# Delta stage: levels whole instead of in halves, leading tokens once per four heads, VectorE's work placed anew

## The reference

```python
q = causal_conv_silu(x @ Wq, conv_q_w, conv_q_b)   # 4 taps in time; k and v the same
g = -jnp.exp(A_log)[None, None, :, None] * jax.nn.softplus(x @ Wfa @ Wfb + dt_bias)
beta = jax.nn.sigmoid(x @ Wb)
q, k = l2norm(q) * SCALE, l2norm(k)

def step(S, inp):
    qt, kt, vt, gt, bt = inp
    S = S * jnp.exp(gt)[..., None]
    vd = (vt - jnp.einsum('bhkv,bhk->bhv', S, kt)) * bt[..., None]
    S = S + kt[..., None] * vd[:, :, None, :]
    return (S, jnp.einsum('bhkv,bhk->bhv', S, qt))
o = o * lax.rsqrt(jnp.mean(o * o, -1) + EPS) * o_norm_w * jax.nn.sigmoid(x @ Wga @ Wgb)
return o.reshape(b, t, D) @ Wo
```

## Time and profile before

| what | value |
|---|---|
| median of 3 runs | 3721.74 us (3715.66 to 3722.37) |
| the profiled execution, its own time | 3717.97 us |
| its span in the profile | 3715.8 us |
| TensorE matmuls busy over the span | 3474.6 us, 94% |
| VectorE busy | 1941.4 us, 52% |
| ScalarE busy | 1427.4 us, 38% |
| GpSimd busy | 125.0 us, 3% |

### The profile page before, as it was taken

The page is one execution under the profiler, slowest core; times in us unless marked ns, Lnnn a source line. Parts: engine busy times, 40 slices in busy tenths (PEclk is TensorE's granted clock), DMA queues, the critical chain, the costliest instruction groups (busy, mean ns, idle before and its releaser), DMA issues. The chain is left out here.

```text
span 3715.8 us, 86134 instructions
## 1 busy us (share of the span) xinstructions
PE 3474.6 (94%) x37416; PEld 1694.5 (46%) x37416; DVE 1941.4 (52%) x3334; ACT 1427.4 (38%) x3313; POOL 125.0 (3%) x457
## 2 busy tenths in 40 slices
PE   6979999996789999999999999999999759999999
PEld 4454444442344544444444444444444435444444
DVE  2131111113778897789878878887888431111111
ACT  1010000001466656666665666566656521000000
POOL 0000000000000000000000000000000000000000
PEclk9979999997989999999999999999999868999999
DMA  4011100003111111121111111111211042000000
GB/s 154 7 57 36 28 0 29 11 0 120 48 31 36 42 50 34 45 66 41 33 56 43 48 50 45 42 37 39 65 39 34 16 154 63 14 15 29 0 12 12
DMA packets 83725, 156.21 MB, mean 42 GB/s; under 512 B 8782, under 2 KB 33998, under 8 KB 79516
## 3 DMA queue, kind: packets, MB, share of 16 engines
q1 hardware_dynamic: 83356, 150.77, 12.3%
HBM read 133.71 MB, written 17.04 MB: 41 GB/s over the span
## 5 line engine op out<-in xcount | busy, mean ns | idle before, releaser
L1333 PE MATMUL psum<-dl_xt,dl_wqkv 128*128 128x512 f32 x1536 | 778.2, 624 | 10.4 <-DVE dl_qkv L977 10.0
L513 DVE SCALAR_TENSOR_TENSOR f_act_g<-psum,f_bup,f_act_g 128x512 f32<-128x512 f32 x96 | 72.1, 751 | 939.4 <-ACT f_act_g L468 939.4
L977 DVE SCALAR_TENSOR_TENSOR dl_qkv<-psum,dl_par,dl_qkv 128x511 f32<-128x511 f32 (+2 forms) x576 | 430.4, 747 | 14.0
L468 ACT ACTIVATE f_act_g<-psum,f_bgate 128x512 f32<-128x512 f32 x96 | 66.0, 687 | 923.1 <-PE psum L411 923.1
L1333 PEld LDWEIGHTS psum<-dl_xt,dl_wqkv 128*128 128x128 f32 x1536 | 257.4, 189 | 250.2 <-issue 212.5
L411 PE MATMUL psum<-xnt_sb,wup 128*128 128x512 f32 x768 | 345.2, 592 | 0.0
L407 PE MATMUL psum<-xnt_sb,wgate 128*128 128x512 f32 x768 | 345.2, 592 | 0.0
L429 PE MATMUL psum<-f_wdown,f_hidden 128*128 128x512 f32 x768 | 344.9, 592 | 0.0
L1340 PE MATMUL psum<-dl_wo,dl_sg 128*128 128x512 f32 x512 | 260.9, 623 | 2.9 <-DVE dl_qkv L977 2.5
L407 PEld LDWEIGHTS psum<-xnt_sb,wgate 128*128 128x128 f32 x768 | 145.9, 190 | 183.7 <-issue 183.7
L411 PEld LDWEIGHTS psum<-xnt_sb,wup 128*128 128x128 f32 x768 | 145.9, 190 | 183.7 <-issue 183.7
(11 more groups left out here) (192 smaller groups left out, 4618.1 us busy)
## 6 DMA issues: line engine op xcount, KB each, us to landing
dl_wqkv<-in_dw_qkv SPq DMA_DIRECT2D x192, 256.0 KB, 2.6
dl_wo<-in_dwo SPq DMA_DIRECT2D x16, 1024.0 KB, 5.2
f_weights_b<-f_weights_by_expert SPq DMA_DIRECT2D x48, 256.0 KB, 6.3
wgate<-in_wgate SPq DMA_DIRECT2D x2, 3072.0 KB, 18.6
wup<-in_wup SPq DMA_DIRECT2D x2, 3072.0 KB, 24.7
f_wdown<-in_wdown SPq DMA_DIRECT2D x2, 3072.0 KB, 13.6
x_sb<-in_x SPq DMA_DIRECT2D x4, 1024.0 KB, 9.3
x_after_experts<-x_sb SPq DMA_DIRECT2D x16, 256.0 KB, 2.0
```

Of the source, the lines that this page charges most:

```text
L977: tap_ = lambda dl: dve.scalar_tensor_tensor(y_[:, dl:TT], ps[:, bank, 0:TT - dl], par[:, h, 4 * a + 3 - dl:4 * a + 4 - dl], y_[:, dl:TT], ...
L1333: last = pe.matmul(ps[:, bank, :], wq[:, n % RING, m, :], xt[:, u // HG % 2, m, :], start=(m == 0), stop=(m == KC - 1))
```

## The change

The level products of a level are issued whole instead of in two halves, at one place of the slot. Their scaling takes all tokens and both parts of `kq` in one instruction (`level_scale`), and the product of the decays is one instruction too (`level_decay`). The wait on `half_level` goes, and `late` counts levels instead of halves. The sums move from the end of slot 8 to its inner place, the cross and corner products to the end of slots 14 and 15. The leading tokens of four heads are added in one instruction after their convolutions (`edges`), for which ScalarE's `silu` now waits; `bnd` is held twice. The series for small arguments has one term less and its threshold is 2^-8 instead of 2^-6. In VectorE's list, the pieces of work get other places before and behind `add_state`; `level_take` of levels 1 to 5 moves from the head of slots 7 to 11 to their tails, `blocks_out` from the tail of slot 11 to the tail of slot 12, and `blocks_in` from the tail of slot 13 to before `add_state` of slot 14.

```diff
-    every, first, second = None, (0, 1), (2, 3)
+    every, quarters = None, (0, 1, 2, 3)
...
-             (6, "states"): [("level", w, 0, first)], (6, "inner"): [("level", w, 0, second)],
-             (6, "split"): [("level", w, 1, first)], (6, "end"): [("level", w, 1, second)],
-             (8, "end"): [("sums", w, 0, every)],
+             (6, "inner"): [("level", w, 0, quarters)], (6, "end"): [("level", w, 1, quarters)],
+             (8, "inner"): [("sums", w, 0, every)],
...
-             (14, "inner"): [("cross", w, 0, first), ("krow", w, 2, every)], (14, "end"): [("cross", w, 0, second)],
-             (15, "inner"): [("vrow", w, 0, every), ("corner", w, 0, first)], (15, "end"): [("corner", w, 0, second)]}
+             (14, "inner"): [("krow", w, 2, every)], (14, "end"): [("cross", w, 0, quarters)],
+             (15, "inner"): [("vrow", w, 0, every)], (15, "end"): [("corner", w, 0, quarters)]}
...
-    if 7 <= sl <= 10 and at in ("inner", "end"):
-        jobs.append(("level", w, sl - 5, first if at == "inner" else second))
+    if 7 <= sl <= 10 and at == "end":
+        jobs.append(("level", w, sl - 5, quarters))
...
                 def silu(u, a, signal):
-                    for j in range(HJ):
-                        wait_read(act, "proj", u, 4 * (1, 0, 2)[a] + j)
+                    act.wait_ge(s["edged"], 3 * u + (2, 1, 3)[a])
                     act.activation(qkv[:, a], qkv[:, a], ACT.Silu).then_inc(signal, 1)
 
...
                     if not late:
-                        if i == 0:
-                            dve.wait_ge(s["bnd_ready"], u + 1)
                         dve.wait_ge(s["tapped"], 12 * u + i + 1)
-                        step(dve.tensor_tensor(y_[:, 0:3], y_[:, 0:3], bnd[:, a, j, :], ALU.add))
                         step(tap_(1))
                         o.done(tap_(2))
                         conv_done[(u, i)] = o.n
...
+                def edges(u, a):
+                    dve.wait_ge(s["bnd_ready"], u + 1)
+                    for j in range(HJ):
+                        wait_read(dve, "proj", u, 4 * (1, 0, 2)[a] + j)
+                    dve.tensor_tensor(qkv[:, a, :, 0:3], qkv[:, a, :, 0:3], bnd(u)[:, a], ALU.add).then_inc(s["edged"], 1)
+
...
-                        o.done(dve.tensor_scalar(poly, w_, -0.25, None, ALU.mult))
+                        o.done(dve.tensor_scalar(poly, w_, 1.0 / 3.0, None, ALU.mult))
                     else:
                         o.wait(mark[("series", u, n - 1)])
-                        ins = dve.scalar_tensor_tensor(poly, poly, (1.0 / 3.0, -0.5, 1.0)[n - 1], w_, ALU.add, ALU.mult)
-                        if n == 3:
-                            ins.then_inc(s["series_done"], 1)
-                        else:
-                            o.done(ins)
+                        o.done(dve.scalar_tensor_tensor(poly, poly, (-0.5, 1.0)[n - 1], w_, ALU.add, ALU.mult))
...
                 def near_zero(u):
                     if u >= 2:
                         dve.wait_ge(s["o_ps"], SLOTS * (u - 1))
-                    o.done(dve.tensor_scalar(flat(kq(u)[:, 1]), flat(sg[:]), 2.0 ** -6, None, ALU.is_lt))
-                    mark[("near", u)] = o.n
+                    o.wait(mark[("series", u, 2)])
+                    dve.tensor_scalar(flat(kq(u)[:, 1]), flat(sg[:]), 2.0 ** -8, None, ALU.is_lt).then_inc(s["series_done"], 1)
...
-                def cut(u, lv, side):
-                    m, hs = 1 << (lv - 1), slice(TT // 2 * side, TT // 2 * side + TT // 2)
-                    segs = lambda ap: ap[:, :, hs].rearrange("p j (n r m) -> p j n r m", r=2, m=m)
-                    return m, segs(qkv[:, KK]), segs(dec)
-
-                def level_early(u, lv, side):
-                    m, kk_, dv = cut(u, lv, side)
-                    nb = TT // (4 * m)
-                    if side == 0:
-                        dve.wait_ge(s["half_level"], (LEVELS + 1) * u + lv + 1)
-                    else:
-                        wait_full(dve, "level", u, lv)
+                def cut(u, lv):
+                    m = 1 << (lv - 1)
+                    segs = lambda ap: flat(ap).rearrange("p (n r m) -> p n r m", r=2, m=m)
+                    return m, HJ * TT // (2 * m), segs(qkv[:, KK]), segs(dec[:])
+
+                def level_scale(u, lv):
+                    m, nb, kk_, dv = cut(u, lv)
+                    wait_full(dve, "level", u, lv)
                     if lv == 1:
                         dve.wait_ge(s["decayed"], 2 * u + 2)
                         dve.wait_ge(s["k_square"], u + 1)
                         wait_full(dve, "level", u, 0)
                     else:
-                        o.wait(mark[("left", u, lv - 1, side)])
-                    for a in range(2):
-                        late = kq(u)[:, a, :, TT // 2 * side:TT // 2 * side + TT // 2].rearrange(
-                            "p j (n r m) -> p j n r m", r=2, m=m)[:, :, :, 1, :]
-                        o.done(dve.tensor_tensor(late, late, dv[:, :, :, 0, 0:1].broadcast_to([P, HJ, nb, m]), ALU.mult))
-                    dve.tensor_tensor(kk_[:, :, :, 0, :], kk_[:, :, :, 0, :], dv[:, :, :, 1, 0:1].broadcast_to([P, HJ, nb, m]),
+                        o.wait(mark[("left", u, lv - 1)])
+                    late = kq(u).rearrange("p a j t -> p a (j t)").rearrange("p a (n r m) -> p a n r m", r=2, m=m)[:, :, :, 1, :]
+                    o.done(dve.tensor_tensor(late, late, dv[:, :, 0, 0:1].unsqueeze(1).broadcast_to([P, 2, nb, m]), ALU.mult))
+                    dve.tensor_tensor(kk_[:, :, 0, :], kk_[:, :, 0, :], dv[:, :, 1, 0:1].broadcast_to([P, nb, m]),
                                       ALU.mult).then_inc(s["late"], 1)
-                    dve.wait_ge(s["late"], 2 * (LEVELS * u + lv - 1) + side + 1)
-                    o.done(dve.tensor_tensor(dv[:, :, :, 0, 0:1], dv[:, :, :, 0, 0:1], dv[:, :, :, 1, 0:1], ALU.mult))
-                    mark[("left", u, lv, side)] = o.n
+
+                def level_decay(u, lv):
+                    m, nb, kk_, dv = cut(u, lv)
+                    dve.wait_ge(s["late"], LEVELS * u + lv)
+                    o.done(dve.tensor_tensor(dv[:, :, 0, 0:1], dv[:, :, 0, 0:1], dv[:, :, 1, 0:1], ALU.mult))
+                    mark[("left", u, lv)] = o.n
...
                             norm_rows(w)
                         if prep and 7 <= sl <= 11:
-                            level_take(w, sl - 6)
-                            level_early(w, sl - 6, 1)
+                            level_scale(w, sl - 6)
                         if conv:
                             convolve(*conv, False)
-                        if before and before[0] == "rows":
-                            add_rows(*before[1:])
+                        if prep and sl == 0:
+                            series(w, 0)
+                        if prep and sl == 1:
+                            series(w, 2)
+                        if prep and sl == 3:
+                            softplus(w)
+                        if post and sl == 4:
+                            o_scale(p, 2)
+                            o_scale(p, 3)
                         if post and sl in (5, 6):
                             gated(p, 2 * sl - 9)
-                        if prep and sl == 3:
-                            choose(w)
-                        if post and sl in (2, 4):
-                            o_scale(p, sl - 2)
-                            o_scale(p, sl - 1)
-                        if prep:
-                            if sl == 11:
-                                whole_decay(w)
-                        if sl == 12 and ahead:
+                        if prep and sl in (5, 6):
+                            decayed(w, (QQ, KK)[sl - 5])
+                        if prep and sl == 12:
+                            norm_tables(w)
+                        if ahead and sl == 12:
                             boundary(w2)
+                        if prep and sl == 14:
+                            blocks_in(w)
 
                         if run:
                             add_state(k, sl)
@@ -1233,37 +1232,34 @@
                             gated(p, 2 * sl - 8)
                         if conv:
                             convolve(*conv, True)
-                        if prep and sl == 13:
-                            blocks_in(w)
-                        if prep:
-                            if sl == 0:
-                                series(w, 0)
-                                series(w, 1)
-                            if sl == 1:
-                                series(w, 2)
-                                near_zero(w)
-                            if sl == 2:
-                                series(w, 3)
-                            if sl == 3:
-                                softplus(w)
-                            if sl == 4:
-                                decayed(w, QQ)
-                            if sl == 5:
-                                decayed(w, KK)
-                            if sl == 6:
```

(49 more changed lines are left out.)

19 lines of the change are left out of this document (10 added, 9 removed).

## The result

The changed kernel takes 3782.76 us (median of 4 runs, 3779.06 to 3790.56) against 3718.7 (3715.29 to 3722.37): ratio 1.0175, interval 1.0154 to 1.0195. The forecast of 3715 and its range (3696 to 3733) are missed by far, on the side to which I gave 0.23. The profiled execution took 3782.61 us, its span is 3780.4.

What follows compares the result with a forecast made beforehand. TensorE's own work was taken as the bound. A unit's -0.1 us gave -1.5 over 15 units; with -4.7 for the first and +0.5 for the last, about -6: 3712 from the profiled run, 3716 as median, said as 3715, range 3696 to 3733.

Steps and rivals of the forecast that it cites:

- the side to which I gave 0.23: Whole kernel: chance 0.23 that the change measures slower, above 3729.2 us.
- the waits that go: TensorE's present waits, mainly for rbuf and ubuf, are all covered by VectorE's new order: -3.9 us a unit.
- the two claims: Slots 8 and 11: TensorE waits for banks that the later level_take releases, 1.9 and 1.5 us a unit.
- case 1: The forecast itself: the two bank claims give back what the covered waits save; 3706 to 3727, chance 0.58.
- cross and blocks: End of slot 14: whole cross asks at 6.5 us, its operand from blocks_in comes at 6.7; +0.2 us a unit.
- rival 3: Slower: blocks_in before add_state leaves cross no reserve, +15 us for each microsecond of lateness; chance 0.22.
- VectorE's prices: VectorE's operations at 1.04 ns an element over a fixed 0.155 us, 1.9 for decay products; 7.4 us a unit saved.
- rival 4: Level-1 scaling of every second word runs at the dear rate, 6.1 us instead of 3.5: 3733, chance 0.06.
- The level products themselves don't change in number.: TensorE's joined level products: only order changes count, +0.2 us a unit, bounds 0 to +0.5.
- TensorE's order: Third and fourth long matmuls parted in slots 7, 9, 10 (+0.2 us each), rejoined in 6 (-0.2); +0.2 a unit taken.
- the first unit: No recurrence runs and TensorE waits for convolutions, so VectorE's saving counts: -4.7 us, bounds -7.4 and 0.

Runs made afterwards that it cites:

- e6: The changed kernel with level products, scalings, decay products and copies into amat put back in halves as before; cross product still whole: 3701.6 us, ratio 0.9954.
- e1: The changed kernel with level_take of levels 1 to 5 back at the head of slots 7 to 11: 3740.7 us, ratio 1.006.
- e11: e6 with the block preparation as before the change and cross in halves inside and at the end of slot 14: 3686.4 us, ratio 0.9909.
- e10: e6 with TensorE's levels 2 to 5 whole at the end of slots 7 to 10, scaling still in halves: 3728.2 us, ratio 1.0023.
- e9: e6 with cross in halves (end of slot 14, slot 15) and corner's halves around slot 15's last long matmul: 3687.0 us, ratio 0.9904.
- e5: The kernel before with the main job's third matmul always ahead of state_step: 3772.7 us, ratio 1.0138.
- e8: e6 with the main job's third matmul always ahead of state_step: 3749.9 us, ratio 1.0072.
- e2: The changed kernel with products of levels 1, 2, 4, 5 and corner in halves around the main job's last matmul: 3794.9 us, ratio 1.0198.
- e3: e1 with level and corner products in halves around the main job's last matmul, for slots 7 to 10: 3771.9 us, ratio 1.0139.
- e12: e9 with scalings and decay products whole as in the change, and level_take behind level_scale at the slot's head: 3801.2 us, ratio 1.0235.
- e7: e1 with levels 2 to 5 whole between the main job's third and fourth matmul instead of behind the fourth: 3793.4 us, ratio 1.0194.

## Why the prediction was wrong

**The miss in numbers.** After is 64 us longer: 54.7 in the 12 units, 5.1 ahead of them and some 5 behind. The 12 units split into `rbuf` and `ubuf` -41.6, `amat` +38.0, "issue" +40.1, other waits +5.7, busy +12.2.

**Right: the waits that go.** "I find every one of the present waits covered": the first two lines of the earlier trace rows have no counterpart in after's 12 units, and e6 shows that the gain can be kept. ScalarE's wait before the gate's sigmoid is gone too:

```profile
1716.50 0.60 ACT L851 ACTIVATE dl_sg<-psum 128x512 f32<-128x512 f32 x1
```

**Right: the two claims.** 1.9 us at slot 8 and 1.5 at slot 11 were forecast, 1.76 and 1.40 are in the timeline above. VectorE's side of slot 8, to be laid beside the earlier trace rows, runs as added up: the copy ends at 1765.15, 4.1 us after the state matmuls of 1761.02, where I had 4.3 (of which 0.1 for signals stood in no row).

```profile
1761.66 0.69 DVE L970 TENSOR_TENSOR dl_alt<-dl_sdec,psum 128x512 f32<-128x512 f32 x1 [1.47 <-PE psum L1309]
1762.27 0.69 DVE L1187 TENSOR_TENSOR dl_xr<-psum,dl_xr 128x512 f32<-128x512 f32 x1
1762.87 1.08 DVE L1066 TENSOR_TENSOR dl_dec<-dl_dec 128x512 f32<-128x512 f32 x1
1763.86 1.29 DVE L1085 COPY_PREDICATED dl_amat<-constants_sb,psum 128x512 f32<-128x512 int32 x1
```

e1 took both away and was 42 us faster, 35.1 of it in the 12 units for 38.0 of waits, so they were worth about what the claims said, and cancelled the covered waits as in case 1.

**Right: cross and blocks.** 0.28 us where I had 0.2; rival 3 did not come.

**Right, but for the sum: VectorE's prices.** To be laid beside the earlier trace rows:

```profile
L1059 DVE TENSOR_TENSOR dl_kq<-dl_kq,dl_dec 128x2048 f32<-128x2048 f32 x59 | 134.3, 2276 | 4.4 <-PE psum L1379 4.4
L1060 DVE TENSOR_TENSOR dl_qkv<-dl_qkv,dl_dec 128x1024 f32<-128x1024 f32 x59 | 71.9, 1218 | 0.0
L1066 DVE TENSOR_TENSOR dl_dec<-dl_dec 128x512 f32<-128x512 f32 x12 | 13.0, 1086 | 0.0
L992 DVE TENSOR_TENSOR dl_qkv<-dl_qkv,dl_bnd 128x12 f32<-128x12 f32 x35 | 6.0, 172 | 4.7
```

2.28, 1.22, 1.09 and 0.17 us against 2.29, 1.22, 1.13 and 0.155 to 0.3. The saving is 70 / 12 = 5.8 us a unit, not 7.4: I multiplied full durations although show two products in 1.29 us, 0.09 less than twice 0.688. The level work alone, between e6 and after, is (1201.02 - 1176.93) / 12 = 2.0 us where I had 3.9, some 0.08 less for each of its 25 operations. It cost nothing here. Level 1, which touches every second word, took 2.28 us like the rest, so rival 4 is out. The Trainium skill's Vector Engine (DVE) Microarchitecture Reference (5.2) has its dearer rate for such hops; the trace doesn't bear it out at a hop of two words.

**Wrong: "The level products themselves don't change in number."** That sentence priced TensorE's side of the joined products at nothing, +0.2 us a unit with bounds 0 to +0.5. This is the step that failed. The number is the same, but 128 small matmuls with their weight loads now go off in one run of 1.2 us, and 24 more behind them. They brought 40 us of gaps that no semaphore explains, and part of the 12 of busy time through the slow clock behind them: e6, with the same 23.9 us at the lower level, is busy 10.1 us more than e11, which has none. The runs show it from both sides: gaps after e10's levels made whole (+15), none at e6's halved ones, and all but 3.8 and 0.5 us gone with the last long runs (e9, e11). With the claims also away, the level work in halves is worth 3740.7 - 3701.6 = 39 us (e1 to e6), 26.6 of it by TensorE's order alone (e10 to e6).

**And it could have been seen.** The first unit of before, where nothing stands between, has two such gaps:

```profile
982.25 1.46 PE L1377 MATMUL psum<-dl_qkv 128*32 128x32 f32 x105 [4.77 <-ACT dl_qkv L828]
986.13 0.50 PE L1377 MATMUL psum<-dl_qkv 128*32 128x32 f32 x20 [2.42 <-issue]
...
986.44 1.63 PE L1383 MATMUL psum<-dl_kq,dl_qkv 128*32 128x32 f32 x104
990.23 1.40 PE L1383 MATMUL psum<-dl_kq,dl_qkv 128*32 128x32 f32 x87 [2.17 <-issue]
```

105 matmuls, then 2.42 us of nothing; 104, then 2.17. I read the waits of that stretch for `qkv` and passed over those marked "issue", because in the middle they sum to 0.9.

**Partly wrong: "TensorE's order".** The parting has about the right unit price (0.2; e5 gives 0.26, e8 0.20). After has two more partings a unit than before (slots 7, 9 and 10 less slot 6), as reckoned; by these prices they are an estimate of 24 x 0.20 to 0.26, 5 to 6 us of the 12.2.

**Wrong sign: the first unit.** I took -4.7 us from VectorE's saving. VectorE did save 10 us there (80.20 to 70.09), and the waits for the convolutions fell from 10.0 to 7.1. But the bank claims stand in this unit too, and without a recurrence to overlap with they are longer, 4.1 and 2.7 us, where before has 1.4 and 0.6; the fourth `wfb` load comes 5.1 us later. I had priced the claims for the 15 other units only. The waits of 912 to 1030 in after:

```profile
PE psum L1379 <- DVE dl_amat L1085: 4.1, 1, 4.1
...
PE psum L1402 <- DVE dl_amat L1085: 2.7, 1, 2.7
```

**What the gaps are.** The edits alone show that the gaps follow the arrangement of small matmuls, and not any operand, bank or engine. The packed trace settles the rest: it has the times of the packets of the instruction queue, which moved 4.83 MB in 295 packets, 16.4 KB each.

```profile
q8 instruction: 295, 4.83, 0.5%
```

The Trainium skill's Trainium Architecture — The Big Picture (The software stack) gives 64 bytes for an instruction. By that (an estimate) a packet holds 256 instructions, as many as the 128 matmuls and 128 loads of a level, used up in 1.2 us. The trace agrees. TensorE's recorded instructions (matmuls, loads and semaphore events) are 76179, or 298 times 256, against the 295 packets. Counted over them, the 37 gaps of after's 12 units stand at multiples of 256 from one another, within two. So do the two gaps above, exactly 256 apart, and all 241 gaps in the 12 units of the 14 kernels. Every one of the 241 also ends 1.2 to 1.7 us after the last packet has landed, whether it is short or long; by chance a matmul falls there in about one case in ten. Four of them, in after:

```
gap                us    packet starts  packet lands  TensorE goes on after
1754.47..1755.80   1.33  1753.40        1754.36       1.44
1773.25..1774.90   1.65  1772.21        1773.63       1.27
1814.78..1816.85   2.07  1814.50        1815.46       1.39
2207.53..2210.99   3.46  2208.66        2209.62       1.37
```

So the supply theory holds: TensorE has used up one packet's instructions and stands until the next is there. In a run of small matmuls a packet is used up soonest. A unit is 16.8 packets (201 in 12 units), so the seam between two of them falls elsewhere in each unit, which fits gaps of 0.3 us in one and 3.5 in another; and 30 of e1's 32 gaps stand at the same instruction of the program as gaps of after.

**What stays open.** What decides when a packet is asked for, and so how long a gap gets, isn't in the trace. Nor is the busy time of e2 and e3 explained: 12 and 19 us more, where one and two more partings a unit are 3 and 6.

## What to carry to other kernels

An engine that is the bound can be slowed by how its own instructions are grouped, though their number and operands stay the same: count the small matmuls between two stretches of long ones, and look for idle time marked "issue" anywhere in the trace of before, also in stretches that don't matter there. Where such gaps stand at multiples of one number of instructions from each other, look at the supply of instructions; moving the copies and the bank claims left these as they were (e1). Halves of a batch have a use that their VectorE overhead hides: they spread the small matmuls, let the scaling of one half run beside the products of the other, and free banks early. When a change bundles several edits, price them apart; here everything but the level work was worth 17 us, with the cross product still whole (e6), and 32 with it in halves (e9, e11), and the joining with its later copies, by which VectorE's busy time looked so much better, cost 81.

## What the runs showed of the hardware

TensorE ran 108 to 128 small matmuls with their loads in 1.14 to 1.3 us and then stood 0.15 to 3.46 us without a semaphore or an operand to wait for. These gaps stand at multiples of 256 recorded instructions from each other, and end 1.2 to 1.7 us after a 16.4 KB packet of the instruction queue has landed (241 of 241, in 14 kernels). Two pairs of long matmuls (1.9 us) between halves of 64 left none at the levels in e6, and at most 0.5 us in before and e12; one pair (1.06 us) left them, before or behind (e3, e7). Four long records as two pairs apart cost 0.20 to 0.26 us more than in a row, 30.8 us over 12 units when done at ten more slots a unit (e5). After a gap of 2.07 us the granted clock was 0.50 from 1818 to 1821, and four long matmuls took 3.11 us instead of 1.98.
